# A four-stage transformer chain on one core: the clip on GpSimd, the second adapter batch by quarters, and a few instructions moved

## The reference

```python
def modifier_block(x, code, ...):                # L0 and L2
    attn = softmax((x @ Wq) @ (x @ Wk).T * 512 ** -0.5)
    attn_out = attn @ (x @ Wv) @ Wp + bp
    cms_out = gelu(attn_out @ cW1 + cb1) @ cW2 + cb2 + one_hot(code)    # hidden width 2048
    modifier = gelu(concat([attn_out, cms_out]) @ mW1 + mb1) @ mW2 + mb2
    return clip(x + cms_out + modifier, 0.0, 1.0)

def adapter(x, role, ...):                       # L1 and L3
    h = gelu(x @ W_down[role] + b_down[role])    # width 256
    y = x + h @ W_up[role] + b_up[role]
    return layernorm(y) * gamma[role] + beta[role]
```

## Time and profile before

| | |
|---|---|
| median of 3 runs | 2107.85 us |
| profiled execution | 2109.29 us, of which the trace spans 2107.6 us |
| granted TensorE clock, mean | 0.998 of full speed |
| TensorE busy | 2075.6 us (98%) |
| VectorE, ScalarE, GpSimd busy | 1588.4, 1096.8, 698.1 us |
| DMA engines, mean load by slice | 80 to 90% at the start, 40% or less over most of the rest |

### The profile page before, as it was taken

How to read it: one execution, slowest core, us unless ns; L and a number is a source line. 1 busy time by engine, 2 the same in 40 slices (tenths; PEclk the granted TensorE clock), 3 DMA queues, 4 the chain that set the end, 5 groups by cost and what they waited for, 6 DMA issues and landing times.

```text
span 2107.6 us, 25014 instructions
## 1 busy us (share of the span) xinstructions
PE 2075.6 (98%) x9128; PEld 1701.4 (81%) x9128; DVE 1588.4 (75%) x1929; ACT 1096.8 (52%) x1625; POOL 698.1 (33%) x686
## 2 busy tenths in 40 slices
PE   9999999999999999999999999999999999999997
PEld 7887888888787887888887888888888888888884
DVE  4368878777867878867777887977686888787776
ACT  5256645454447654544554755544444666354444
POOL 1244416674002331766100332455400032165510
PEclk9999999999999999999999999999999999999999
DMA  8895444543222424444403222422130422421111
GB/s 295 238 240 143 132 120 113 133 119 105 94 73 78 153 75 137 115 113 101 137 21 133 88 71 76 105 60 61 46 125 1 150 70 98 122 61 52 58 60 40
DMA packets 183417, 221.93 MB, mean 105 GB/s; under 512 B 10224, under 2 KB 148208, under 8 KB 178688
## 3 DMA queue, kind: packets, MB, share of 16 engines
q1 hardware_dynamic: 175776, 184.58, 27.0%
q0 software_dynamic: 6144, 29.47, 7.8%
q10 hardware_dynamic: 1376, 6.29, 0.8%
HBM read 199.33 MB, written 62.91 MB: 124 GB/s over the span
## 4 chain that ended last, share of the span: by engine, by line
PE 88%; DVE 8%; ACT 2%; DMA 1%; issue 1%; SPq 0%; ACTq 0%; DVEq 0%
PE bank L857 29%; PE bank L859 29%; PE bank L858 29%; DVE ring L1737 1%; DVE lsum L2184 1%; DVE xa L1774 1%; DMA fold_staging<-fold_w 1%; ACT ring L1278 1%; DMA stage<-ready_up 1%; DVE pc L2009 1%; PE bank L1242 1%; DVE xs L2189 0%; DVE xs L2142 0%; DVE xs L2174 0%; DVE vc L1746 0%
## 5 line engine op out<-in xcount | busy, mean ns | idle before, releaser
L1737 DVE TENSOR_TENSOR ring<-stage,ring 128x1024 fp32r<-128x1024 f32 (+1 forms) x288 | 356.2, 1247 | 97.5 <-ACT ring L1278 97.3
L857 PE MATMUL bank<-xa,ring 128*128 128x512 f32 x1016 | 396.1, 390 | 2.2 <-DVE xs L2142 2.1
L859 PE MATMUL bank<-xa,ring 128*128 128x512 f32 x1016 | 395.3, 389 | 0.0
L858 PE MATMUL bank<-xa,ring 128*128 128x512 f32 x1016 | 395.3, 389 | 0.0
L1278 ACT ACTIVATE ring<-stage 128x1024 fp32r<-128x1024 f32 (+1 forms) x288 | 271.9, 963 | 118.0 <-PE bank L859 71.5
L857 PE MATMUL bank<-ph_hi,ring 128*128 128x512 f32 x808 | 317.0, 392 | 4.5 <-DVE pc L2009 1.8
L859 PE MATMUL bank<-ph_hi,ring 128*128 128x512 f32 x808 | 314.5, 389 | 0.0
L858 PE MATMUL bank<-ph_lo,ring 128*128 128x512 f32 x808 | 314.5, 389 | 0.0
L857 PE MATMUL bank<-vc,ring 128*128 128x512 f32 x704 | 274.3, 390 | 0.2
L859 PE MATMUL bank<-vc,ring 128*128 128x512 f32 x704 | 273.9, 389 | 0.0
L858 PE MATMUL bank<-vc,ring 128*128 128x512 f32 x704 | 273.9, 389 | 0.0
(11 more groups left out here) (195 smaller groups left out, 3608.6 us busy)
## 6 DMA issues: line engine op xcount, KB each, us to landing
stage<-ready_up SPq DMA_DIRECT2D x40, 896.0 KB, 5.2
stage<-mod_w SPq DMA_DIRECT2D x112, 256.0 KB, 3.4
stage_pair<-ready_pair SPq DMA_DIRECT2D x12, 1792.0 KB, 10.7
stage<-mod_w SPq DMA_DIRECT2D x28, 512.0 KB, 5.0
ready_up<-ready_up POOLq DMA_DIRECT2D x100, 128.0 KB, 5.1
ready_up<-cms_w SPq DMA_DIRECT2D x98, 128.0 KB, 3.6
ready_pair<-cms_w SPq DMA_DIRECT2D x42, 256.0 KB, 6.2
stage<-folded SPq DMA_DIRECT2D x16, 512.0 KB, 6.2
```

Source lines behind the costliest of these rows:

```text
L857: pe.matmul(dst, lh, rh, start=start and n == 0, stop=False, skip_group_check=not start)
L858: pe.matmul(dst, lh, rl, start=False, stop=False, skip_group_check=not start)
L859: done = pe.matmul(dst, ll, rh, start=False, stop=n == last, skip_group_check=not start)
L1737: dve.tensor_tensor(ring_part(key, 1), staged(key), f32(ring_part(key, 0)), ALU.subtract).then_inc(w_lo, 1)
```

## The change

It has five parts.

1. The clip leaves VectorE. GpSimd does it after its last work of the modifier, one tile at a time, and signals ScalarE. `mod_end` on VectorE becomes: four additions of batch 0, four low parts of batch 0, an addition of batch 1, then in turn an addition and a low part of batch 1.
2. The down products of batch 1 in `adapt` run with the contraction outermost, so that each of the four input tiles is used for both products before the next one is waited for.
3. The low part of U0 moves behind the eight additions of the up products.
4. In `attend`, the split of P moves behind the V tiles and the transposed tiles on both engines, and ScalarE no longer waits for all four V tiles. The softmax of batch 1 moves ahead of one `norm_rstd` and one `norm_affine`.
5. The residual DMA of batch 1 is issued as two halves with a semaphore each; the high part of T4 waits for the first, the low part for the second.

```diff
-        res_added = [sem(f"res_added{b}") for b in range(GROUP)]
+        res_first, res_second = sem("res_first"), [sem(f"res_second{half}") for half in range(2)]
@@ GpSimd
-                pool.wait_ge(added, added_at(r, CH - 1, b, KT - 1))
-                pool.dma_start(xs[:, b, :, :], pc[:, b, :, :], accum_op=ALU.add).then_inc(res_added[b], 16)
+                if b == 0:
+                    pool.wait_ge(added, added_at(r, CH - 1, b, KT - 1))
+                    pool.dma_start(xs[:, b, :, :], pc[:, b, :, :], accum_op=ALU.add).then_inc(res_first, 16)
+                    return
+                for half in range(2):
+                    m = 2 * half
+                    pool.wait_ge(added, added_at(r, CH - 1, b, m + 1))
+                    pool.dma_start(xs[:, b, m:m + 2, :], pc[:, b, m:m + 2, :], accum_op=ALU.add).then_inc(res_second[half], 16)
...
                 sum_ahead(r, SLOTS - 1)
+                for b in range(GROUP):
+                    for m in range(KT):
+                        pool.wait_ge(added, added_at(r, SLOTS - 1, b, m))
+                        pool.tensor_scalar(xs[:, b, m, :], xs[:, b, m, :], 0.0, 1.0, ALU.max, ALU.min).then_inc(z_ready, 1)
@@ TensorE, adapt
+                    if b == 1:
+                        for k in range(KT):
+                            pe.wait_ge(z_lo, r * GROUP * KT + KT * b + k + 1)
+                            for m in range(MC):
...
+                                pe.matmul(dst, wh, half_hi(vc, b, k), start=k == 0, stop=False)
+                                pe.matmul(dst, wh, half_lo(vc, b, k), start=False, stop=False)
+                                done = pe.matmul(dst, wl, half_hi(vc, b, k), start=False, stop=k == KT - 1)
+                                if k == KT - 1:
+                                    done.then_inc(ada_done, 1)
+                        continue
@@ ScalarE, attend
-                act.wait_ge(att_done, m0 + M_V1 + KT)
-                split_hi((r, "P"))
                 plain_hi(m0 + M_V1, lambda m: bank[m][:, :], lambda m: half_hi(vc, 1, m))
                 plain_hi(m0 + M_T0, lambda m: bank[4 + m][:, :], lambda m: ph_hi[:, m, :])
+                split_hi((r, "P"))
                 exps(r, 1, bank[0:4])
@@ ScalarE, cms_build
-                act.wait_ge(res_added[1], 16 * (r + 1))
+                act.wait_ge(res_second[0], 16 * (r + 1))
@@ VectorE, attend
-                split_lo((r, "P"))
                 plain_lo(s0 + S_V1, lambda m: bank[m][:, :], lambda m: half_hi(vc, 1, m), lambda m: half_lo(vc, 1, m))
                 if r:
                     norm_scale(before, 0)
                 plain_lo(s0 + S_P0, lambda m: bank[4 + m][:, :], lambda m: ph_hi[:, m, :], lambda m: ph_lo[:, m, :])
+                split_lo((r, "P"))
+                softmax(r, 1, m0 + M_S1, bank[0:4])
                 if r:
                     norm_rstd(before, 1)
                     norm_affine(before, 0)
-                softmax(r, 1, m0 + M_S1, bank[0:4])
-                if r:
                     norm_scale(before, 1)
                     norm_affine(before, 1)
@@ VectorE, slot8
+                dve.wait_ge(res_second[1], 16 * (r + 1))
                 operand_lo(vc, T4, raw[:, 2:4, :], cms_hi, t0 + BUILT[T4], cms_lo)
@@ VectorE, mod_end
-                for b in range(GROUP):
-                    for m in range(KT):
-                        down_add(r, n, b, m)
-                        dve.wait_ge(added, added_at(r, n, b, m))
-                        dve.tensor_scalar(xs[:, b, m, :], xs[:, b, m, :], 0.0, 1.0, ALU.max, ALU.min).then_inc(z_ready, 1)
-                    for k in range(KT):
...
+                for m in range(KT):
+                    down_add(r, n, 0, m)
+                for k in range(KT):
+                    z_tile_lo(0, k)
+                down_add(r, n, 1, 0)
+                for m in range(1, KT):
+                    down_add(r, n, 1, m)
+                    z_tile_lo(1, m - 1)
+                z_tile_lo(1, KT - 1)
@@ VectorE, adapt
-                    if more and b == 0:
-                        split_lo((r + 1, "U0"))
+                if more:
+                    split_lo((r + 1, "U0"))
```

More of the change, by code:

```diff
@@ L1216, in adapt @@
                     pe.wait_ge(w_lo, W_AT[r, f"d{b}"])
+                    if b == 1:
+                        for k in range(KT):
+                            pe.wait_ge(z_lo, r * GROUP * KT + KT * b + k + 1)
+                            for m in range(MC):
+                                wh, wl = plain_w(f"d{b}", k * HC + m * P, k * HC + (m + 1) * P)
+                                dst = bank[MC * b + m][:, :]
+                                pe.matmul(dst, wh, half_hi(vc, b, k), start=k == 0, stop=False)
[4 more added lines that the diff above has]
+                        continue
                     for m in range(MC):
@@ L1405, in cms_build @@
                 act.wait_ge(cms_t, t0 + CMS_T[T3])
-                act.wait_ge(res_added[0], 16 * (r + 1))
+                act.wait_ge(res_first, 16 * (r + 1))
                 operand_hi(vc, T3, raw[:, 0:2, :], cms_hi)
@@ L1886, in seven_add @@
                 else:
-                    dve.wait_ge(res_added[b], 16 * (r + 1))
+                    if b == 0:
+                        dve.wait_ge(res_first, 16 * (r + 1))
+                    else:
+                        dve.wait_ge(res_second[m // 2], 16 * (r + 1))
                 minus = q in (Q5, Q7, Q4)
@@ L2119, in mod_end, with z_tile_lo @@
                 n = SLOTS - 1
-                for b in range(GROUP):
-                    for m in range(KT):
-                        down_add(r, n, b, m)
-                        dve.wait_ge(added, added_at(r, n, b, m))
-                        dve.tensor_scalar(xs[:, b, m, :], xs[:, b, m, :], 0.0, 1.0, ALU.max, ALU.min).then_inc(z_ready, 1)
-                    for k in range(KT):
-                        dve.wait_ge(z_hi, r * GROUP * KT + KT * b + k + 1)
-                        dve.tensor_tensor(half_lo(vc, b, k), xs[:, b, k, :], f32(half_hi(vc, b, k)),
-                                          ALU.subtract).then_inc(z_lo, 1)
+                def z_tile_lo(b, k):
+                    dve.wait_ge(z_hi, r * GROUP * KT + KT * b + k + 1)
+                    dve.tensor_tensor(half_lo(vc, b, k), xs[:, b, k, :], f32(half_hi(vc, b, k)), ALU.subtract).then_inc(z_lo, 1)
+                for m in range(KT):
[7 more added lines that the diff above has]
+                z_tile_lo(1, KT - 1)
             def adapt(r, more):
```

## The result

| | median, us | runs | ratio to before, 95% interval |
|---|---|---|---|
| before | 2108.06 | 5 (2107.24 to 2110.55) | |
| after | 2121.73 | 5 (2119.26 to 2125.81) | 1.0069 [1.0055, 1.0082] |

The changed kernel is 0.7% slower, 13.7 us, where 11.6 us less was forecast. 2121.73 us is 25 us from the forecast and 17.7 us above the range. The side was that of the second rival, which had 8 chances in 100; its figure (2112 to 2118 us) was still too low. The profiled execution is the one of 2121.73 us, with a span of 2120.0 us (before: 2107.6 us) and a granted clock of 0.997.

The account below looks back on a forecast made before the run. TensorE, busy 2075.6 of 2107.6 us, was taken as the bound, matmuls unchanged, with a few waits to remove. Savings of 8.2 + 1.4 + 2.0 = 11.6 us from 2107.85 gave 2096.5 us, range 2095 to 2104.

Parts of the forecast that it names:

- the second rival: Clip on GpSimd at the two-input price or dearer, from 1.3 us: 15 to 21 us lost, 2112 to 2118; chance 0.08.
- The V low parts: In attend, TensorE's wait for V low parts (line 1746), 1.44 us in each of four rounds, goes.
- the softmax: In attend, TensorE's wait for batch 1's softmax (line 1756), 1.15 us in three rounds, goes.
- the passage: Between rounds, TensorE's wait for batch 1's up product additions: 0.86 us lost, 0.65 won each time, 2.0 in three.
- The layer norm behind the softmax: In attend, VectorE's layer norm pieces pushed behind batch 1's softmax end in time by 0.1 us: costs 0, at most 0.3.
- The quarters of d1: In the adapter, d1's products with contraction outermost make the fourth gelu, and the chain to the passage's addition, 0.55 us later.
- The residual: Batch 1's residual DMA in two halves: no gain seen, 0 us.
- The clip's price: One 512-column clip on GpSimd taken as 0.75 us, between estimates of 0.59 and 1.16, with 1.29 from above.
- the first rival: A GpSimd clip of 0.85 to 1.2 us: adapters give back 0.2 to 3 us each, 2097 to 2107; chance 0.26.
- The schedule with a given price: In the adapter, ScalarE's u1 and gelus next in line: 0 lost at 0.75 us, 0.1 to 0.8 to spare.
- take turns: In the adapter, VectorE's low parts and GpSimd's clips block each other; about 8 us of stall per us of clip from 0.83.

Follow-up runs that it names:

- e3: The kernel before with part 4 alone (P split behind the V tiles, batch 1's softmax moved ahead), clip on VectorE: 2098.37 us, ratio 0.9950.
- e4: The kernel before with part 3 alone (low part of U0 behind the eight additions), clip on VectorE: 2105.91 us, ratio 0.9983.
- e6: The kernel before with parts 3 and 4 alone, clip on VectorE, d1 whole, residual in one piece: 2096.35 us, ratio 0.9942.
- e1: The kernel after with the clip back on VectorE, right behind each addition, all else as after: 2097.33 us, ratio 0.9943.
- e10: The kernel before with part 2 alone (d1 with the contraction outermost), clip on VectorE: 2109.57 us, ratio 1.0006.
- e8: The kernel before with part 5 alone (batch 1's residual DMA as two halves), clip on VectorE: 2108.14 us, ratio 0.9998.
- e5: The kernel after with the clip's upper bound left out, one ALU operation per element on GpSimd: 2113.59 us, ratio 1.0021.
- e9: The kernel after with each GpSimd clip made by two instructions of 256 columns: 2131.68 us in its one run.
- e7: The kernel after without part 2 (batch 1's down products whole again), clip on GpSimd: 2125.78 us, ratio 1.0083.
- e2: The kernel before with only the clip moved to GpSimd, low parts in the old order: 2136.24 us, ratio 1.0126.

## Why the prediction was wrong, by its steps

**The V low parts, the softmax and the passage: right.** The terms of part 4 were 8.2 + 1.4 = 9.6 us and that of part 3, without the 0.55 of part 2, 3 x 0.86 = 2.6, in all 12.2. Measured: 10.5 (e3), 3.6 (e4), 12.2 (e6). All ten waits, 5.0, 3.0 and 2.1 us in sum, are absent from after and from e6. In the kernel after the second transposes of round two now follow the attended tiles with no wait:

```profile
635.94 0.39 PE L869 MATMUL bank<-ph_hi,vc 128*128 128x512 f32 x1
636.63 1.91 PE L924 MATMUL bank<-ident,pc 128*128 128x128 f32 x16
638.30 0.47 PE L869 MATMUL bank<-ph_hi,vc 128*128 128x512 f32 x1
```

**The layer norm behind the softmax: right, with a margin that held.** VectorE of the kernel after, the row that ends that layer norm and the next:

```profile
641.12 1.91 DVE L2228 TENSOR_SCALAR xs<-xs,avec 128x512 f32<-128x512 f32 x4
642.94 2.47 DVE L1771 TENSOR_TENSOR xa<-bank,xa 128x512 fp32r<-128x512 f32 x4
```

The last affine ends at 643.0 and the first low part (642.94 + 0.69) is there at 643.63; TensorE wants it 1.67 + 5.44 us behind 636.63, at 643.74, and its next product starts at 643.87 with no idle time shown. The margin was given as 0.1 us and is about that. It made no wait in after, e1, e3 or e6.

**The quarters of d1: right.** 0.56 us for 0.55 (e10), and in e1, where parts 2 and 3 are together, 0.25 us is lost at each passage, for 0.22 worked out (557.6 - 557.38). **The residual: right** (e8).

**The clip's price: wrong, and this is the step that failed.** It stood at 0.75 us, and with it the adapters' stall at nothing; the figure came from half the two-input slope and, from below, from a 128-column instruction of another kind. It measured 1.92, with 5.6 us of stall a round. The error was in the direction of the bound: the two-input addition of 512 columns, 1.29 us, was called the upper end, because a clip reads one input less. Nor was it the only row with 512 columns: the trace of before has seven more lines of GpSimd additions of that size, with means of 1.36 to 1.98 us, and none of their rows is below 1.26. The runs show that reading less did not make it cheaper. One input and one ALU operation cost 1.49 us (e5), above two inputs and one operation; the second operation adds 0.43. Per column the clip takes 3.34 ns, the two-input addition 2.16. That each element takes two ALU operations was said, as a point for the first rival, and put into no bound; the price from above should have been open. The Trainium skill's figure (GPSIMD Engine Reference, 3.1) is 769 ns for 512 elements in its best case of a loop, and it sets a two-input addition above that; that the loop has one input was the forecast's reading. This instruction does not do that here: the measured 1487 ns for one operation is twice the figure, and the order of the two is reversed.

**The schedule with a given price: right in place, half wrong in size.** The forecast named ScalarE's u1 and the gelus behind it as next in line, and with them the up product, and that is the wait of 1.81 us. It had low parts and clips take turns, from a single row of 1.20 us. In the adapters of after they don't: four clips of batch 0 take 7.58 us on end, and the low parts that run within them 0.69 us each, as they do alone. In e5 VectorE shows two that are stretched:

```profile
538.43 1.08 DVE L2151 TENSOR_TENSOR vc<-xs,vc 128x512 fp32r<-128x512 f32 x1 [0.16 <-ACT vc L1650]
...
540.53 0.81 DVE L2151 TENSOR_TENSOR vc<-xs,vc 128x512 fp32r<-128x512 f32 x1 [0.43 <-ACT vc L1650]
```

Both begin just behind the start of a clip (538.35 and 540.19), as the row of 1.20 us did behind its addition, and both end some 1.15 us behind that start, at most 0.4 us late; low parts begun 0.5 us or more behind it are not held. The other way round the hold is longer, and the trace of before had it. A GpSimd addition of 512 columns that takes 1.29 us on line 768 takes 1.67 on line 780, where all 28 begin 0.15 to 0.17 us behind the start of a low part and so with 0.52 us of it left:

```profile
L780 POOL TENSOR_TENSOR raw<-raw x28: 1662/1669/1679, 334.8 to 2023.5; 128x512 f32<-128x512 f32 x28
...
444.44 0.69 DVE L1931 SCALAR_TENSOR_TENSOR ph_lo<-raw,ph_hi 128x512 fp32r<-128x512 f32 x1
444.61 1.67 POOL L780 TENSOR_TENSOR raw<-raw 128x512 f32<-128x512 f32 x1 [1.45 <-DVE ph_lo L1933]
```

The Trainium skill has it that the later of two such instructions waits for the whole of the other (SBUF — State Buffer, Who interferes with whom). These rows agree for most of the way when the GpSimd instruction is the later one (0.38 us of 0.52 here, 0.25 of 0.39 in e9), and disagree when VectorE's is: one begun in the middle of a clip isn't held at all, and one begun at its start not for the clip's 1.49. In after no clip begins while a low part runs, so none is stretched. With turns, the forecast's 8 us of stall a round for each us of clip from 0.83 on would give 8.7 us a round at 1.92; without them it gave 1.5 a round at 1.29. Measured: 5.6 a round at 1.92 and 3.1 at 1.49 at full clock (6.6 and 4.1 by the times, which have the clock in them).

**The second rival** had the right mechanism, with its threshold of 1.3 us passed. It gave 2112 to 2118 because it stopped at 1.5 us a clip. That e5, at 1.49, lies inside that at 2113.59 is in part luck: the rival's stall for 1.5 us was 5.4 us a round, where 3.1 was measured, and about 1.1 a round came from the clock, which was not in the sum. For 1.92 us it lacked the rest of the price and the clock, 1.6 us in the profiled execution of after.

**Account.** The adapters of after lose 24.0 us and those of e1 none; at the three passages e1 loses 0.8 us and after none. That leaves 23.2 us. The spans differ by 26.3 us; the other 3 us are spread over starts under 0.1 us late and stretches outside the adapter, and were not followed. A wait behind a late weight load of the first round, 1.6 us in after (the `raw_odd` row), is 0.2 to 1.5 us in several others, 1.5 in e6 with the clip on VectorE, and so is not the clip's.

## What to carry to other kernels

Before an elementwise operation moves to another engine, take its price there from a row with the same operation, the same number of ALU operations and the same columns; if the trace has none, leave the price open above instead of capping it by a row that looks dearer, and measure it by itself. Moving work off an engine at 75%, with TensorE at 98%, gained nothing here: the clip on VectorE was covered whole, and on GpSimd it became a link of the chain that feeds TensorE, eight times a round at 1.92 us. And before two versions are compared by their times, look at the clock in each round: between after and e7 it makes up the difference, and the stall at full clock is the same. The gain of this change lay in the order of instructions alone: two moves in `attend` and one behind the additions (e6) are worth 12 us.

## What the runs showed of the hardware that was not expected

- GpSimd's clip of 128x512 fp32 takes 1.92 us with two ALU operations and 1.49 with one, more than its two-input addition of the same size (1.29). The extra operation is 0.43 us. VectorE needs 0.43 us for the same clip.
- TensorE's clock was at the 1.2 GHz level for some 5 to 11 matmuls (0.43 us apart) behind the waits of an adapter, none of them over 2 us: in the profiled executions, in all four rounds of e2 and e9, in three of four in e5 and e7, in one of four in after, in none of before, e1 and e6, which have no wait there. e5 waits less than after (7.9 us listed in its adapters against 15.9) and its clock fell more often, so here the sum of the waits does not say how often; what does is not shown. Such stalls cost more than they add up to, by 1.4 us or more for each round in which the clock fell, and the runs of after scatter by 6.5 us, those of before by 3.3.
- Which of two engines is held depends on which begins first. VectorE's low parts, two inputs in SBUF, take 0.1 to 0.4 us more when they begin 0.1 to 0.3 us behind the start of a clip (e5), and nothing more from 0.5 us on (after). GpSimd instructions that begin while such a low part runs take 0.25 us more with 0.39 us of it left (e9, line 860) and 0.38 more with 0.52 left (before, line 780).
